# Two layer norms moved behind their matrix products: centred weights, raw rows in, inverse deviation on the results

## The reference

```python
def reference(x, ctx, ...):                            # x, ctx: 32 x 128 x 1024, float32
    x = x + autocorrelation(layernorm(x), ctx)         # stage A: spectra, top 9 lags, softmax, aggregation
    h = layernorm(x)                                   # stage B: (h - mean) / sqrt(var + eps), this is norm 1
    p, i = top_k(softmax(h @ W_router.T), 2); combine = one_hot(i) * p / sum(p)     # 8 experts
    x = x + h @ W_base.T + b_base + (h @ A_stack * combine) @ B_stack * 2
    x = x + window_attention(layernorm(x), ctx)        # norm 2, then stage C
    h = layernorm(x)                                   # norm 3
    gates = softmax(top2(h @ Wr.T))                    # 4 experts
    return x + sum(gates * (h @ A @ B)) * 4
```

## Time and profile before

| what | value |
|---|---|
| median of 3 runs | 1869.83 us (1869.39 to 1873.03) |
| span of the profiled execution | 1871.1 us |
| which of the three times belongs to the profiled execution | not shown |
| TensorE matmul busy | 1712.3 us, 92% of the span |
| VectorE busy | 1575.8 us, 84% |
| ScalarE busy | 1372.6 us, 73% |
| GpSimd busy | 1028.3 us, 55% |
| length of nearly every step from 158 us to 1753 us | 54.98 us |

### The profile page before, as it was taken

The page is one execution under the profiler, slowest core; times in us unless marked ns, Lnnn a source line. Parts: engine busy times, 40 slices in busy tenths (PEclk is TensorE's granted clock), DMA queues, the critical chain, the costliest instruction groups (busy, mean ns, idle before and its releaser), DMA issues. The chain is left out here.

```text
span 1871.1 us, 48299 instructions
## 1 busy us (share of the span) xinstructions
PE 1712.3 (92%) x19296; PEld 1078.5 (58%) x19296; DVE 1575.8 (84%) x4726; ACT 1372.6 (73%) x2121; POOL 1028.3 (55%) x934
## 2 busy tenths in 40 slices
PE   3689999999999999999999999999999999999875
PEld 1355566666556656556666655666665566565543
DVE  5778898888888888889888888988888888888853
ACT  4277777878777787877777887778787777878753
POOL 1555556556555656655556655555565556566542
PEclk7899999999999999999999999999999999999995
DMA  5111110111010111101011110101110101111000
GB/s 208 34 35 36 35 46 25 47 46 46 24 47 27 44 46 47 47 24 47 24 47 46 47 38 33 46 25 47 46 46 24 47 28 43 46 47 35 2 12 24
DMA packets 20977, 77.82 MB, mean 42 GB/s; under 512 B 2704, under 2 KB 2960, under 8 KB 20240
## 3 DMA queue, kind: packets, MB, share of 16 engines
q1 hardware_dynamic: 20752, 74.72, 11.7%
HBM read 57.94 MB, written 16.78 MB: 40 GB/s over the span
## 5 line engine op out<-in xcount | busy, mean ns | idle before, releaser
L586 PE MATMUL pb<-w_base_h,even_words 128*128 128x512 f16 x1024 | 324.8, 379 | 0.0
L1438 POOL TENSOR_TENSOR p_hl<-sc,p_hl 128x512 f16<-128x512 f32 x128 | 164.2, 1283 | 206.6 <-ACT p_hl L764 206.6
L877 ACT ACTIVATE q_diag<-sc,par 32x512 f32<-32x512 f32 x384 | 269.4, 717 | 8.0
L1483 POOL TENSOR_TENSOR sc<-sc,sc_rec 128x512 f32<-128x512 f32 x128 | 134.4, 1050 | 216.8 <-DVE sc_rec L1245 216.6
L586 PE MATMUL pb<-w_base_l,even_words 128*128 128x512 f16 x512 | 193.9, 379 | 0.0
L473 PE MATMUL pa<-xn_a,tab 128*128 128x512 f32 x384 | 180.5, 606 | 4.6 <-ACT xn_a L764 4.6
L660 PEld LDWEIGHTS pc<-sc_t,v_diag 128*128 128x128 f16 x6144 | 170.2, 97 | 20.6 <-DVE sc_t L1252 6.0
L660 PE MATMUL pc<-sc_t,v_diag 128*128 128x32 f16 x6144 | 173.9, 177 | 5.6 <-DVE sc_t L1252 5.6
L637 PE MATMUL pc<-k_h,q_diag 128*128 128x32 f16 x2048 | 169.1, 177 | 0.0
L638 PE MATMUL pc<-k_l,q_diag 128*128 128x32 f16 x2048 | 168.4, 177 | 0.0
L639 PE MATMUL pc<-k_h,q_diag 128*128 128x32 f16 x2048 | 168.4, 177 | 0.0
(11 more groups left out here) (170 smaller groups left out, 5008.1 us busy)
## 6 DMA issues: line engine op xcount, KB each, us to landing
x_a<-in_x SPq DMA_DIRECT2D x32, 512.0 KB, 3.6
x_res<-in_ctx_in SPq DMA_DIRECT2D x32, 512.0 KB, 4.4
x_res<-in_x SPq DMA_DIRECT2D x32, 512.0 KB, 4.5
out<-rows_c SPq DMA_DIRECT2D x32, 512.0 KB, 2.9
v_diag<-in_base_w SPq DMA_DIRECT2D x4, 1024.0 KB, 10.4
q_diag<-in_ra SPq DMA_DIRECT2D x1, 544.0 KB, 14.1
q_diag<-in_b SPq DMA_DIRECT2D x1, 512.0 KB, 15.8
q_diag<-in_b SPq DMA_DIRECT2D x2, 256.0 KB, 17.0
```

Of the source, the lines that this page charges most:

```text
L586: mm(pb[:, h, :], rows[:, cols], weights[:, j, h * HALF:(h + 1) * HALF], start=(j == 0 and m == 0), stop=False)
L877: nc.scalar.activation(q_diag[rows, blocks, col:col + QB], source, ACT.Copy, scale=par[rows, a:a + 1]).then_inc(qd_out.sem, 1)
L1438: g_.tensor_tensor(part[:, :, :, LO], sc[:, g % 2, :, :], part[:, :, :, HI], ALU.subtract)\
L1483: g_.tensor_tensor(sc[:, g % 2, :, :], sc[:, g % 2, :, :], sc_rec[:, blocks].unsqueeze(2).to_broadcast([P, GB, KEYS]), ALU.mult)\
```

## The change

Norms 1 and 3 are no longer applied to the rows. TensorE transposes the raw rows `x_b` and `rows_c`, and the products run over them with weights whose column mean over the 1024 features has been subtracted. The result is multiplied by the inverse deviation where it leaves PSUM: `gates` (L1187), `b_base` (L1150) and `c_result` (L1268) take a per-partition factor `rs_w` or `rs_y` in place of the constant 1/256 or 1. Once, before element 0 reaches stage B, TensorE multiplies the float32 weights with a matrix of 1/1024 (`weight_means`) and VectorE subtracts the result (`centre_weights`), ahead of `split_weights`. GpSimd's `root` has one more small product for norms 1 and 3, and `b_bias` waits for the transposes in place of `xn_b`. The last transpose of the values waits for the squares of ScalarE, which now use the buffer alone.

```diff
--- before.py
+++ after.py
@@ -212,7 +212,8 @@
         xt_c = sc_t[:, :, :, :].rearrange("p a n k -> p (a n k)")
-        xn_c = v_t[1]
+        squares_c = v_t[1]
+        ones_mean = rows_c[:, 0:P]
@@ -253,6 +256,8 @@
         pb_all, pc_all = flat(pb[:, :, :]), flat(pc[:, :, :])
+        ra0_mean = pb[:, 0, 0:E0 + P]
+        ra1_mean = pb[:, 0, E0 + P:E0 + P + E1 + E1 * RANK]
         MID_AT = 256
@@ -376,6 +385,7 @@
         WEIGHTS_SPLIT = SPLITS + 3
+        CENTRED = SPLITS + 2
@@ -549,10 +559,28 @@
-            def rows_to_features(b, n, ln, source, place):
-                pe.wait_ge(ln_out[ln].sem, ln_out[ln].after(b))
+            def weight_means():
+
+                pe.wait_ge(ones_set.sem, 1)
+                pe.wait_ge(w_in.sem, 16 * (SPLITS + 4))
+                ra0_rows = ra0_f32.rearrange("p (k n) -> p k n", k=KT)
+                for j in range(KT):
+                    mm(ra0_mean, ones_mean, ra0_rows[:, j, :], start=(j == 0), stop=(j == KT - 1))
+                for j in range(KT):
+                    mm(ra1_mean, ones_mean, w_ra1[:, j, :], start=(j == 0), stop=(j == KT - 1))
+                for h in range(2):
+                    for j in range(KT):
+                        at = j * D + h * HALF
+                        last = mm(pc[:, h, :], ones_mean, base_f32[:, at:at + HALF],
+                                  start=(j == 0), stop=(j == KT - 1))
+                last.then_inc(w_mean.sem, 1)
+
+            def rows_to_features(b, n, source, place):
                 if n == 0:
-                    if not first(b):
+                    pe.wait_ge(x1_out.sem, x1_out.after(b))
+                    if first(b):
+                        pe.wait_ge(w_centred.sem, 2)
+                    else:
                         pe.wait_ge(ql_out.sem, ql_out.after(b - 1))
@@ -722,7 +750,7 @@
                 if live(3):
-                    rows_to_features(i - 3, 1, 3, xn_c, pc)
+                    rows_to_features(i - 3, 1, rows_c, pc)
                     c_router(i - 3)
@@ -737,7 +765,7 @@
                 if live(1):
-                    rows_to_features(i - 1, 0, 1, xn_b, pb)
+                    rows_to_features(i - 1, 0, x_b, pb)
                 if live(2):
@@ -755,6 +783,7 @@
                     pe.wait_ge(const_set.sem, CONSTS_SET)
+                    weight_means()
                 step(i, i % 2, during(i))
@@ -801,7 +830,8 @@
                 if n == 2:
-                    act.wait_ge(tr_x[0].sem, tr_x[0].after(b))
+                    if not first(b):
+                        act.wait_ge(mm_qq.sem, mm_qq.after(b - 1))
                 else:
@@ -920,6 +950,7 @@
                 for part in range(SPLITS):
+                    act.wait_ge(w_centred.sem, part + 3)
                     cols = slice(part * KT * D // SPLITS, (part + 1) * KT * D // SPLITS)
@@ -977,7 +1008,7 @@
                 if live(3):
-                    spread(i - 3, 3, rows_c, xn_c, 1 - odd)
+                    spread(i - 3, 3, rows_c, squares_c, 1 - odd)
                 if live(2):
@@ -1040,11 +1071,12 @@
                     .then_inc(ln_part[n].sem, 1)
-                v.tensor_scalar(mv[n][:, 0:1], ln_sum[n][:, :], 1.0 / D, None, ALU.mult).then_inc(ln_mean[n].sem, 1)
+                if n == 2:
+                    v.tensor_scalar(mv[n][:, 0:1], ln_sum[n][:, :], 1.0 / D, None, ALU.mult)\
+                        .then_inc(ln_mean[n].sem, 1)
             def normalise(b, n, rows, place):
-                if n in (2, 3):
-                    dve.wait_ge(ln_mean[n].sem, ln_mean[n].after(b))
+                dve.wait_ge(ln_mean[n].sem, ln_mean[n].after(b))
                 dve.wait_ge(ln_rs[n].sem, ln_rs[n].after(b))
@@ -1128,13 +1160,10 @@
-            def b_norm_rows(b, n, slot):
-                if n == 1:
-                    if not first(b):
-                        dve.wait_ge(mm_qq.sem, mm_qq.after(b - 1))
-                else:
-                    dve.wait_ge(tr_x[0].sem, tr_x[0].after(b))
-                normalise(b, n, x_b[:, :] if n == 1 else x_c[:, slot, :], xn_b)
+            def b_norm_rows(b, slot):
+                if not first(b):
+                    dve.wait_ge(mm_qq.sem, mm_qq.after(b - 1))
+                normalise(b, 2, x_c[:, slot, :], xn_b)
@@ -1145,9 +1174,10 @@
                 dve.wait_ge(bias_added.sem, bias_added.after(b))
+                dve.wait_ge(ln_scale[1].sem, ln_scale[1].after(b))
                 if not early(b):
                     dve.wait_ge(x3_out.sem, x3_out.after(b - 2))
-                v.scalar_tensor_tensor(out=x_c[:, slot, :], in0=pb_all, scalar=1.0 / W_SCALE, in1=x_b[:, :],
+                v.scalar_tensor_tensor(out=x_c[:, slot, :], in0=pb_all, scalar=rs_w[1][:, :], in1=x_b[:, :],
                                        op0=ALU.mult, op1=ALU.add, accum_out=ln_sum[2][:, :])\
@@ -1172,7 +1202,7 @@
                 elif not first(b):
-                    dve.wait_ge(tr_x[1].sem, tr_x[1].after(b - 1))
+                    dve.wait_ge(ln_mv[3].sem, ln_mv[3].after(b - 1))
                 v.transpose(v_t[odd], v_pad[:, odd * QB:odd * QB + D]).then_inc(vt_out.sem, 1)
@@ -1184,7 +1214,11 @@
                 dve.wait_ge(mm_ra[n].sem, mm_ra[n].after(b))
-                v.tensor_scalar(lg[n][:, 0:experts], source[:, 0, 0:experts], [1.0 / W_SCALE, 1.0][n], None,
+                if n == 0:
+                    dve.wait_ge(ln_scale[1].sem, ln_scale[1].after(b))
+                else:
+                    dve.wait_ge(ln_rs[3].sem, ln_rs[3].after(b))
+                v.tensor_scalar(lg[n][:, 0:experts], source[:, 0, 0:experts], [rs_w[1], rs_y[3]][n][:, :], None,
                                 ALU.mult).then_inc(lg_out[n].sem, 1)
@@ -1259,14 +1293,25 @@
-            def c_norm_rows(b):
-                normalise(b, 3, rows_c[:, :], xn_c)
-
             def c_result(b, h):
...
                 cols = slice(h * HALF, (h + 1) * HALF)
-                v.scalar_tensor_tensor(out=rows_c[:, cols], in0=pc[:, h, :], scalar=1.0 / W_SCALE,
+                dve.wait_ge(ln_scale[3].sem, ln_scale[3].after(b))
+                v.scalar_tensor_tensor(out=rows_c[:, cols], in0=pc[:, h, :], scalar=rs_w[3][:, :],
                                        in1=rows_c[:, cols], op0=ALU.mult, op1=ALU.add).then_inc(x4_out.sem, 1)
+
+            def centre_weights():
+
+                dve.wait_ge(const_in.sem, CONSTS_IN)
+                dve.wait_ge(w_mean.sem, 1)
+                quarter = KT // SPLITS
+                base_rows = base_f32.rearrange("p (k n) -> p k n", k=KT)
+                centred = [(ra0_f32.rearrange("p (k n) -> p k n", k=KT), ra0_mean),
+                           (w_ra1[:, :, :], ra1_mean)]
+                centred += [(base_rows[:, part * quarter:(part + 1) * quarter, :], pc_all) for part in range(SPLITS)]
+                for rows, column_mean in centred:
+                    v.tensor_tensor(rows, rows, column_mean.unsqueeze(1).to_broadcast(list(rows.shape)),
+                                    ALU.subtract).then_inc(w_centred.sem, 1)
@@ -1310,6 +1355,7 @@
                 if first(i - 0):
+                    centre_weights()
                     split_weights(range(WEIGHTS_SPLIT))
@@ -1326,12 +1372,10 @@
                 if live(1):
-                    b_norm_rows(i - 1, 2, 1 - odd)
+                    b_norm_rows(i - 1, 1 - odd)
                 if live(0):
...
                     a_products(i, 1)
-                if live(2):
-                    c_norm_rows(i - 2)
                 if live(0):
@@ -1349,8 +1393,6 @@
                     c_scores(i - 1, 0)
-                if live(0):
-                    b_norm_rows(i, 1, odd)
                 if live(1):
@@ -1377,6 +1419,8 @@
             v.memset(minus_one[:, :], -1.0).then_inc(power_set.sem, 1)
+            v.memset(unscaled[:, :], 1.0 / W_SCALE).then_inc(power_set.sem, 1)
+            v.memset(ones_mean, 1.0 / D).then_inc(ones_set.sem, 1)
             v.memset(ninth[:, :, :], GONE).then_inc(const_set.sem, 1)
@@ -1407,6 +1451,10 @@
                 g_.tensor_tensor(rs_y[n][:, :], rs_v[n][:, :], rs_power[:, :], ALU.pow).then_inc(ln_rs[n].sem, 1)
+                if n in (1, 3):
+                    pool.wait_ge(ln_rs[n].sem, ln_rs[n].after(b))
+                    g_.tensor_tensor(rs_w[n][:, :], rs_y[n][:, :], unscaled[:, :], ALU.mult)\
+                        .then_inc(ln_scale[n].sem, 1)
                 if n == 0:
@@ -1416,7 +1464,8 @@
                     pool.wait_ge(const_in.sem, CONSTS_IN)
-                pool.wait_ge(ln_out[1].sem, ln_out[1].after(b))
+                pool.wait_ge(tr_x[0].sem, tr_x[0].after(b))
+                pool.wait_ge(ln_bn[1].sem, ln_bn[1].after(b))
                 g_.tensor_tensor(x_b[:, :], x_b[:, :], bias_base[:, :], ALU.add).then_inc(bias_added.sem, 1)
@@ -1507,7 +1556,7 @@
                 if live(0):
-                    pool.wait_ge(ln_rs[1].sem, ln_rs[1].after(i))
+                    pool.wait_ge(ln_scale[1].sem, ln_scale[1].after(i))
                 if live(1):
@@ -1535,13 +1584,13 @@
```

(10 more changed lines are left out.)

## The result

The changed kernel takes 1882.49 us (median of 4 runs, 1882.33 to 1882.72), the kernel before beside it 1871.43 us (median of 4; one of them, at 2011 us, is far off and left out of the ratio, and the other three have a median of 1869.83). The ratio is 1.0061, 95% interval [1.0046, 1.0076]: slower by 11 to 13 us, where 1881 us was forecast. The span of the profiled execution grew from 1871.1 to 1880.6 us, by 9.5.

A forecast was written before the change was run, and what follows sets the result against it. ScalarE's gapless queue, not the 92% busy TensorE, was taken to bound part of each step and hide the removals. Preparation +15.1, factors +1.8 and drain -5.3 gave +11.6 us on 1869.8: 1881 us, range 1870 to 1889.

The forecast's parts named there:

- The removals cost or give nothing in a step: Steady step: removing two VectorE passes and TensorE's waits gains nothing, hidden by 19.5 us of ScalarE; uncovered, 0.78 us.
- +0.06 us a step for the column as a factor: Steady step, L1150: a per-partition factor lengthens a pass on the chain, 31 times, +1.8 us (bounds 0 and 2.1).
- a_corr's wait from 0.50 to about 0.9: Steady step, TensorE: `a_corr` stays the next late instruction and its wait for VectorE grows to about 0.9 us.
- The late bias add: Rival, GpSimd in every step: it pushes value blocks past 1.08 us of idle time; 1890 us at 0.3 a step, chance 0.06.
- Preparation, +15.1 us: Before element 0's products: first product 22.4 us later, less 6.1 and 1.2 given back, +15.1 us (bounds 11 and 19).
- the slow start: TensorE's means start at a slow clock, costing 0.8 us (bounds 0.2 and 2.2).
- Two instructions a call: TensorE's means: a float32 call is two instructions, so 16 base calls are 32 at 0.44, 14.1 us.
- The split, 15.6 us: VectorE's `split_weights` up to the first product: 17.3 us less 1.7 us of one held-up pass, 15.6 us.
- The given-back part: Fill of element 0: 6.1 us back because GpSimd's `v_diag` clearing no longer delays norm 1's normalise, 1.2 from the clock.
- The drain, -5.3 us: Last elements: norm 3 3.3 us, norm 1 1.8, norm 3 of the element before 0.4, less 0.2; bounds -3.5 and -6.5.
- The sum: Whole kernel: +15.1 + 1.8 - 5.3 = +11.6 us, added to the median of 1869.8 us, 1881 us.
- TensorE decides: Rival, steady step: TensorE sets the step and gets its waits back, 0.78 us in 30 steps, 1856 us; chance 0.08.

The follow-up runs named there:

- run 6: Changed kernel with ScalarE issuing the three second-half query blocks after `v_im` and `v_re` instead of ahead: 1872.29 us, ratio 1.0003.
- run 7: Kernel before with ScalarE issuing the three second-half query blocks after `v_im` and `v_re`: 1868.40 us, ratio 0.9981.
- run 9: Changed kernel with ScalarE's two evictions of the router's features put ahead of the value block before them: 1892.93 us, ratio 1.0113.
- run 4: Changed kernel with norm 1 put back as before, so norm 3 alone is moved: 1868.20 us, ratio 0.9982.
- run 5: Changed kernel with norm 3 put back as before, so norm 1 alone is moved: 1884.30 us, ratio 1.0066.
- run 8: Changed kernel with base means ahead of the long context product and the base centred ahead of the softmax: 1874.63 us, ratio 1.0017.
- run 2: Kernel before with only the means and the centring added: 1893.54 us, ratio 1.0117.
- run 3: Kernel before with only GpSimd's memset of `v_diag` moved behind the bias of element 0: 1863.87 us, ratio 0.9958.
- run 1: Changed kernel without its preparation (no column means, no centring, so mean subtraction is not computed): 1857.42 us, ratio 0.9926.
- run 10: Changed kernel with early means, plus ScalarE reordered: values before query blocks, router's features earlier, first exponential behind `v_re`: 1867.57 us, ratio 0.9978.
- run 11: Kernel before with memset behind the bias, plus ScalarE reordered: values before query blocks, router's features earlier, first exponential behind `v_re`: 1882.40 us, ratio 1.0055.
- run 12: Norm 3 alone moved, memset behind the bias, `v_im` and `v_re` ahead of second-half query blocks, first exponential behind two of these: 1851.34 us, ratio 0.9891.

## Why the prediction was right, point by point

- **The removals cost or give nothing in a step: right in the mechanism, off in size.** ScalarE's queue hides them; runs 6, 7 and 9 show it. But that queue was not quite full. VectorE's transpose and ScalarE's value blocks behind it, before the change and after it:
```profile
1104.09 1.24 DVE L1176 STREAM_TRANSPOSE p_hl<-v_pad 128x1024 f32<-128x1024 f32 x1
1105.36 2.13 ACT L764 ACTIVATE v_diag<-p_hl 32x1024 f32<-32x1024 f32 x2
```
```profile
1113.92 1.23 DVE L1206 STREAM_TRANSPOSE p_hl<-v_pad 128x1024 f32<-128x1024 f32 x1
1115.83 2.10 ACT L793 ACTIVATE v_diag<-p_hl 32x1024 f32<-32x1024 f32 x2
```
  Before, the blocks started as the transpose ended (1105.33), 11.71 us into the step. With the normalise of norm 3 gone from between the products the transpose ends 0.75 us sooner, the blocks start at 11.61 behind their own queue alone, and from the copy `mid_t` on the gain is 0.15 to 0.18. Run 4 gives 0.16 us a step, run 5 none. That this is the path of the 0.17 us is read from the timelines; no run tried the two places apart.
- **+0.06 us a step for the column as a factor: the size of the pass is right, the term is not.** L1180 takes 1284 instead of 1225 ns. It is hidden: L1292 cannot start before TensorE's output product ends (1107.19 in the step shown), and starts 3.03 us into the step, before the change 3.02. Norm 1 alone (run 5) has steps of 54.97. Together the two points make -0.17 instead of +0.06 us, some 7 us over the steps. The slow steps, which I did not foresee, gave most of that back: each is 1.5 us above an ordinary one, 4.5 in all.
- **a_corr's wait from 0.50 to about 0.9: right,** 0.94 in the step shown. The late bias add waits for the transposes 61.6 us in sum and delays nothing: GpSimd still idles 0.39 us ahead of the scores' normalisation, and starts it 27.78 us into the step, before the change 27.95. That rival is out.
- **Preparation, +15.1 us: the means and the centring.** The means end at 48.8 instead of 50.4: they start 0.7 us sooner, and the slow start costs about 0.3 us (2.29 us for the 16 instructions that took 2.02 in run 8) instead of 0.8. Two instructions a call at 0.44 us is right (13.95 us for 32). The centring takes 10.7 us as counted. That it is never held up was no test, since GpSimd idles for 27.12 us up to 65.51; but VectorE's L1103 and L1105, which also read PSUM, run beside the memset of `v_diag` (91.34 to 98.27) in their usual 1.23 and 1.21 us. The Trainium skill ("SBUF — State Buffer", "Who interferes with whom") says that a VectorE pass with at most one SBUF input, outside the two-port modes, does not contend with GpSimd, and the trace agrees.
- **The split, 15.6 us, and the fill behind it.** The split takes 15.65 us as forecast, though not for the reason given: before the change two of its passes were held up, not one (the w_ra pass took 3.20 us, now 1.28), and one of the base passes still is (4.21 us, beside GpSimd's L1474, which makes the low half of the context). The first product comes 20.96 us later instead of 22.4, and `a_corr` at 94.79 with its two instructions in 0.49 us, as forecast (95). By the end of element 1 only 12.2 us are left, the step after the fill having run at a granted clock of 0.97 instead of 0.94. The given-back part is confirmed by runs 2 and 3: it comes from no product or norm of the change, only from a memset that no longer holds up the normalise.
- **The drain, -5.3 us: too much by 3.3.** Norm 3 of the last element came as counted: from the start of its last residual pass to the last result pass 12.60 us instead of 15.81. Norm 1's part was more than lost to the clock. TensorE waited 3.2 us for `xn_b` in both kernels, kept its clock before, and fell to the lower one in the changed kernel (here before, then after):
```profile
1810.90 1.98 PE L473 MATMUL pb<-xn_b,w_att 128*128 128x512 f32 x4 [3.16 <-DVE xn_b L1049]
1813.21 1.10 PE L560 MATMUL pc<-ident,p_hl 128*128 128x128 f32 x8 [0.33 <-DVE p_hl L1049]
```
```profile
1821.13 3.78 PE L483 MATMUL pb<-xn_b,w_att 128*128 128x512 f32 x4 [3.21 <-DVE xn_b L1081]
1824.71 1.91 PE L588 MATMUL pc<-ident,rows_c 128*128 128x128 f32 x8
```
  The granted clock in the 2 us from the product's start is 1.00 before and 0.50 after. That is 2.6 us. The change does not force it: in run 1 the same product, after the same 3.21 us, took 1.98 us at the full clock. But the clock fell by the start of this product in 6 of the 7 kernels with norm 1 moved and in 1 of the 7 without (in two more of these, within it), one execution of each, so whether the change makes it likelier is open.
- **The sum** was right to 1.5 us, and that it was so close is luck: errors of both signs met, the steps 2.4 us better and the fill with its first step 2.9 us better than their terms, the drain 3.3 us worse, so that the spans give +9.5 us instead of +11.6. No term for steps that fall to the lower clock was in it.
- **TensorE decides** (the rival at 1856 us) is wrong for this order of ScalarE's queue. Runs 10 and 11 come to its price, 0.81 us a step, but half of it through ScalarE's wait for the transposes and not through waits that TensorE gets back.

## What to carry to other kernels

Removing a wait pays only if the engine that ends last at the next meeting point also comes sooner; the cheap test is to move that engine's work, not to remove more of the waiting. Fixed work ahead of a pipeline is paid once per launch, by as much as it delays the first element (21.3 us here, for 28.5 us of work), so divide that by the number of steps before trading it against a per-step gain: 21.3 us over 32 elements asks for 0.67 us a step, and this change gave 0.17 (under the other orders tried, 0.41 and 0.81). Take a change apart: the half that needs 2.6 us of preparation work (norm 3) was a small gain, the half that needs the other 26 us a loss.

## What the runs showed of the hardware

- TensorE's granted clock fell for some 3 us in steady steps of all six kernels in which it waits 1.36 us ahead of the router (runs 1, 6, 4, 8, the changed kernel and run 12: in 2, 3, 4, 3, 3 and 10 of 29 steps), and in no steady step of the eight in which it waits 0.95 or 0.74 us there. 24 of the 25 falls begin 1.2 to 2.3 us after the start of the router's products, behind that wait; one, in run 8, begins at `a_corr`, before which TensorE had waited 1.29 us. Each fall costs 1.5 to 2.0 us, so a longer wait can go with a price beyond its length. It is not the wait alone, since most steps with the same wait keep the clock. Why run 12, with the same wait in a shorter step, fell ten times, mostly in every third step, is open.
- After 3.15 to 3.22 us of waiting ahead of the same product in the drain, TensorE was at the lower clock by the product's start in 7 of the 14 kernels, fell within the product in two (runs 3 and 7), and kept the full clock in five.
- A GpSimd memset of 6.92 us turned VectorE's normalise of 0.81 us into 7.38 us when it started 0.09 us earlier (the kernel before, runs 2, 4 and 7); moved behind the next GpSimd operation it did not (run 3: 0.81 us).
- A per-partition column in place of a constant costs a scalar_tensor_tensor pass 59 ns at 1024 elements (1225 to 1284; 1283 with norm 1 alone moved, 1225 with norm 3 alone) and 60 ns at 512 (L1300, 686 to 746). Means of single lines wander less than that: L1292, whose form did not change, went from 1282 to 1259 ns.
